# Second graph layer: the last 42 of 154 groups of edge tiles are gathered by POOL and summed by one-hot products

## The reference

```python
h = jnp.maximum(_layernorm(x, axis=-1), 0.0)
# _gcn_conv
dinv = rsqrt(degree)                      # degree of each node
h = h @ W_gcn
msg = h[src] * (dinv[src] * dinv[dst])[:, None]
features = segment_sum(msg, dst)          # sum over the edges of each dst
x = x + relu(features @ W1 + b1) @ W2 + b2
```

## Time and profile before

| | us |
|---|---|
| median of 3 runs | 7662.83 (7657.39 to 7690.72) |
| the profiled execution, its own time | 7676.02 |
| its span in the trace | 7674.2 |
| stages 1 (0 to 1130), 2 (to 5884), 3 (to 6103) | 1130, 4754, 219 |
| stage 4 (6103 to 7614) | 1511 |
| stage 5 (7614 to 7674) | 60 |

### The profile page before, as it was taken

One profiled execution on the slowest core, in us unless ns is written; L12 is line 12 of the kernel. 1 busy time (PEld: TensorE's weight loads), 2 busy tenths in 40 slices (PEclk: granted clock), 3 DMA queues, 4 the chain that ended last, 5 costly groups with the idle time before them and its releaser, 6 DMA issues. The chain is left out here.

```text
span 7674.2 us, 127785 instructions
## 1 busy us (share of the span) xinstructions
PE 5336.5 (70%) x34546; PEld 3643.4 (47%) x34546; DVE 4190.5 (55%) x13388; ACT 4709.8 (61%) x11022; POOL 3260.8 (42%) x3411
## 2 busy tenths in 40 slices
PE   7544436666666666666666666666657999999998
PEld 5211114444444444444434444444445677777777
DVE  4555564444444344444444444444445699999997
ACT  3454535555555555555555555555554499999997
POOL 3555545555555555555555555555555200000000
PEclk7555556666666666666676666666675599999998
DMA  4333322223222222232223222322232111111111
GB/s 158 105 97 93 96 72 71 70 69 87 69 69 71 85 70 69 70 88 71 71 70 88 70 71 71 86 72 69 70 87 69 37 68 68 68 68 68 68 68 69
DMA packets 315566, 586.38 MB, mean 76 GB/s; under 512 B 129522, under 2 KB 185858, under 8 KB 306546
## 3 DMA queue, kind: packets, MB, share of 16 engines
q1 hardware_dynamic: 202882, 324.53, 13.3%
q0 software_dynamic: 103344, 158.83, 9.8%
q10 hardware_dynamic: 8640, 94.84, 3.1%
HBM read 426.94 MB, written 150.87 MB: 75 GB/s over the span
## 5 line engine op out<-in xcount | busy, mean ns | idle before, releaser
L977 POOL DMA_INDIRECT gbuf<-a_tab,idxb x2688 | 2601.7, 968 | 2157.9 <-ACT idxb L968 1048.7
L1077 DVE TENSOR_TENSOR pre<-psum,gbuf 128x384 f32<-128x384 f32 x806 | 449.3, 557 | 2203.0 <-remote 1388.9
L1183 PE MATMUL psum<-x_all 128*128 128x294 bf16 x1260 | 477.8, 379 | 1367.1 <-ACT x_all L1194 860.9
L1064 PE MATMUL psum<-rhs,lhs 128*128 128x96 f32 x6448 | 1317.1, 372 | 27.0 <-ACT lhs L1038 19.8
L1064 PEld LDWEIGHTS psum<-rhs,lhs 128*128 128x128 f32 x6448 | 1202.7, 278 | 130.2 <-issue 55.7
L1108 PE MATMUL psum<-msg,oh 128*128 128x388 f32 x1612 | 1062.1, 755 | 216.2 <-ACT msg L1085 171.0
L1085 ACT ACTIVATE msg<-pre 128x384 f32<-128x384 f32 x806 | 419.9, 521 | 1282.4 <-DVE pre L1077 741.8
L1892 PE MATMUL psum<-x_all 128*128 128x294 bf16 x5208 | 1059.5, 289 | 51.6 <-DVE x_all L1885 16.2
L1183 PEld LDWEIGHTS psum<-x_all 128*128 128x128 bf16 x1260 | 142.2, 113 | 1925.1 <-issue 1032.5
L1884 DVE TENSOR_SCALAR x_all<-x_all,dstrel 128x588 bf16<-128x588 f16 x2604 | 959.4, 368 | 88.6
L1118 ACT ACTIVATE x_all<-psum 32x97 f32<-32x97 f32 x3224 | 776.7, 241 | 335.2 <-remote 245.8
(11 more groups left out here) (230 smaller groups left out, 7499.6 us busy)
## 6 DMA issues: line engine op xcount, KB each, us to landing
adj_tab<-x_all ACTq DMA_DIRECT2D x60, 1543.5 KB
gbuf<-a_tab,idxb POOLq DMA_INDIRECT x3224
x_all<-dst_row SPq DMA_DIRECT2D x806, 64.0 KB
x_all<-attr_parts SPq DMA_DIRECT2D x807, 36.0 KB
x_all<-attr_parts SPq DMA_DIRECT2D x403, 72.0 KB
x_all<-adj_tab SPq DMA_DIRECT2D x30, 945.0 KB
nf<-adj_tab SPq DMA_DIRECT2D x30, 882.0 KB
spilled<-gbuf SPq DMA_DIRECT2D x134, 192.0 KB
```

The costliest lines, as they stand in the source:

```text
L977: g.indirect_dma_start(gbuf[:, k % 4, t, :], None, a_tab[:, :], bass.IndirectOffsetOnAxis(ap=idxb[:, k % 4, t:t + 1], axis=0)).then_inc(g_ ...
L1064: ins = pe.matmul(ps_m(k)[:, t, :], lhs[:, k % 2, t * TILE:(t + 1) * TILE], rhs[:, k % 2, :], start=True, stop=True)
L1183: pe.matmul(bank[7][:, 0:HB], low_e[:, n % 2, :], key_e[:, n % 2, b * HB:(b + 1) * HB], start=True, stop=True).then_inc(n_mm, 1)
```

## The change

The last 42 groups (882 tiles, of which 872 hold edges: 218 supertiles) are no longer counted. They are the "tail". Of the other 112 groups 28 are early and 84 late, and an early group is multiplied during two of every three late groups (`w % 3 >= 1`).

* Stage 3: ACT copies each chunk's table rows from PSUM to `wide_rows` (`layer_row`), SP stores them in DRAM as `t_tab` (`layer_row_store`), and DVE's `layer_t` reads that copy. Keys are made for 2352 tiles in place of 3234.
* Stage 4: POOL gathers each tail tile's 128 rows of 32 values from `t_tab` into a ring of four supertiles (`tail_gather`). Every 8 counted tiles (`TSTEP`), DVE writes a supertile's one-hots of 32 columns (`tail_onehot`), PE multiplies the gathered rows by them in four float32 products (`tail_product`), and DVE adds 32 x 32 sums to `sT` (`tail_add`).

```diff
+TAIL = 42
+TR = 4
-        self.early = [g for g in range(4, self.NG, 5)][:self.SV // EARLY]
-        self.late = [g for g in range(self.NG) if g not in self.early]
+        self.counted = self.NG - TAIL
+        self.early = [g for g in range(3, self.counted, 4)][:self.SV // EARLY]
+        self.late = [g for g in range(self.counted) if g not in self.early]
...
+        def layer_row(act, i, k):
+            act.wait_ge(p_hid.sem, p_hid.at(c))
+            act.wait_ge(p_t.sem, p_t.at(c - 2))
+            if c >= 2:
+                act.wait_ge(o_t[k], 16 * i)
+            act.activation(t_row[:, k, :, :], ps_t(k), ACT.Copy).then_inc(p_row.sem, 1)
...
+        TSTEP = ND * GT // NTB
+        def tail_gather(g, b):
+            if b >= TR:
+                g.wait_ge(t_mm, b - TR + 1)
+            first = (d.first + b) * SUP
+            for t in range(SUP):
+                g.indirect_dma_start(g_rows[:, b % TR, t, :], None, t_tab[:, :],
+                                     bass.IndirectOffsetOnAxis(ap=src_i[:, first + t:first + t + 1], axis=0)).then_inc(t_land[b % TR], 16)
+
+        def tail_onehot(dve, b):
+            if b >= 2:
+                dve.wait_ge(t_mm, b - 1)
+            dve.tensor_tensor(o_tail[:, b % 2, :, :], iota_w.unsqueeze(1).to_broadcast([P, SUP, W]),
+                              dstrel[:, d.first + b, :].unsqueeze(2).to_broadcast([P, SUP, W]),
+                              ALU.is_equal).then_inc(t_oh, 1)
+
+        def tail_product(pe, b):
+            n = b * TSTEP
+            pe.wait_ge(t_oh, b + 1)
+            pe.wait_ge(t_land[b % TR], 16 * SUP * (b // TR + 1))
+            if n >= 3:
+                pe.wait_ge(a_ok, n - 2)
+            for t in range(SUP):
+                ins = pe.matmul(ps_tail(b), g_rows[:, b % TR, t, :], o_tail[:, b % 2, t, :], start=(t == 0), stop=(t == SUP - 1))
+            ins.then_inc(t_mm, 1)
+
+        def tail_add(dve, b):
+            n = b * TSTEP + 3
+            base = dve.value_load(base_i[:, d.first + b:d.first + b + 1], min_val=0, max_val=N - 1)
+            dve.wait_ge(t_mm, b + 1)
+            dve.wait_ge(a_ok, b * TSTEP + 1)
...
+            dve.tensor_tensor(nodes_of, nodes_of, ps_tail(b), ALU.add).then_inc(t_add, 1)
...
         def tile_counts(pe, n):
             pe.wait_ge(e_oh, n + 1)
             if n >= 3:
                 pe.wait_ge(a_ok, n - 2)
+                if tails_added(n + 1):
+                    pe.wait_ge(t_add, tails_added(n + 1))
...
+                    for b in range(NTB):
+                        tail_gather(g, b)
...
-                            if w % 4 >= 2 and w // 4 < NE:
-                                early_sums(pe, w // 4, (w % 4 - 2) * GT + j)
+                            if w % 3 >= 1 and w // 3 < NE:
+                                early_sums(pe, w // 3, (w % 3 - 1) * GT + j)
```

More of the change, by code:

```diff
@@ L58, in __init__ @@
         self.TD = GT * self.NG
-        self.early = [g for g in range(4, self.NG, 5)][:self.SV // EARLY]
-        self.late = [g for g in range(self.NG) if g not in self.early]
+        self.counted = self.NG - TAIL
+        self.early = [g for g in range(3, self.counted, 4)][:self.SV // EARLY]
+        self.late = [g for g in range(self.counted) if g not in self.early]
+        self.first = self.counted * GT // SUP
+        assert self.counted * GT % SUP == 0
+        self.NTB = self.SV - self.first
         self.NE, self.ND = len(self.early), len(self.late)
@@ L1398, in _ @@
                         ins = pe.matmul(bank[6 + b][:, 0:len(gs) * GT].rearrange("p (n j) -> p n j", j=GT), ones[0:1, :],
-                                        dst_e[0:1, gs[0]:gs[-1] + 1:5, :], start=True, stop=True)
+                                        dst_e[0:1, gs[0]:gs[-1] + 1:4, :], start=True, stop=True)
                     ins.then_inc(n_first, 1)
@@ L1508, in gnn_kernel @@
         t_rest = pre[:, :, :, 0:H]
-        KP = -(-TD // NCH)
-        key_f = dflat[:, 0:TD]
-        lo_f = src_i[:, 0:TD].bitcast(FP32)
+        TK = GT * d.counted
+        KP = -(-TK // NCH)
+        key_f = dflat[:, 0:TK]
+        lo_f = src_i[:, 0:TK].bitcast(FP32)
+        t_row = wide_rows
+        p_row = signal("p_row", 2)
+        o_t = [sem("o_t0"), sem("o_t1")]
         hi_i = rhs[:, :, :].rearrange("p b c -> p (b c)")[:, 0:KP].bitcast(I32)
@@ L1523, in tiles_of @@
         def tiles_of(c):
-            return range(c * KP, min((c + 1) * KP, TD))
+            return range(c * KP, min((c + 1) * KP, TK))
         def ps_mixed(k):
@@ L1691, in after @@
                 dve.wait_ge(q_t, 8 * c + n)
-            dve.tensor_copy(parts[0], ps_t(k)).then_inc(q_t, 1)
+            dve.tensor_copy(parts[0], t_row[:, k, :, :]).then_inc(q_t, 1)
             dve.tensor_scalar(hi, src_i[:, tiles], 7, None, ALU.logical_shift_right).then_inc(q_t, 1)
             after(1)
-            dve.tensor_tensor(rest, ps_t(k), parts[0], ALU.subtract).then_inc(q_t, 1)
+            dve.tensor_tensor(rest, t_row[:, k, :, :], parts[0], ALU.subtract).then_inc(q_t, 1)
             dve.tensor_scalar(src_i[:, tiles], src_i[:, tiles], P - 1, None, ALU.bitwise_and).then_inc(q_t, 1)
@@ L1721, in step @@
                     layer_store(sp, i, k)
-                layer.run(sp, step, 0)
+                    layer_row_store(sp, *layer.earlier(i, k, 4))
+                layer.run(sp, step, 4)
                 sp.wait_ge(p_t.sem, p_t.at(NCH - 1))
@@ L1726, in _ @@
                 sp.dma_start(nf[N % P:N % P + 1, pad:pad + C // 2], zrow[:, 0:C // 2]).then_inc(o_zero, 16)
-                sp.wait_ge(o_zero, 16)
+                for k in range(2):
+                    sp.wait_ge(o_t[k], 16 * ((NCH + 1 - k) // 2))
+                sp.dma_start(t_tab[N:N + 1, :], zrow[:, 0:H]).then_inc(o_zero, 16)
+                sp.wait_ge(o_zero, 32)
                 sp.wait_ge(o_res, 16 * NCH)
@@ L1803, in _ @@
                 act.activation(wc[:, H:H + 1], ident[0:C + 1, C:C + 1], ACT.Copy)
-                for x in (p_deg, p_col, p_own):
+                for x in (p_deg, p_col, p_own, p_row):
                     x.start(act)
@@ L1813, in step @@
                     layer_own(act, *layer.earlier(i, k, 7))
+                    layer_row(act, *layer.earlier(i, k, 7))
                 layer.run(act, step, 7)
@@ L1870, in gnn_kernel, with tails_added, late_added @@
         BJ = 7
+        NTB = d.NTB
+        TSTEP = ND * GT // NTB
+        g_rows = sq[:, :, :, :].rearrange("p b t c -> p (b t c)")[:, 0:TR * SUP * H].rearrange("p (b t c) -> p b t c", b=TR, t=SUP)
+        o_tail = oh[:, 2:4, :, :]
+        t_land = [sem(f"t_land{k}") for k in range(TR)]
+        t_oh = sem("t_oh")
+        t_mm = sem("t_mm")
+        t_add = sem("t_add")
+        def tails_added(n):
+            return min(NTB, max(0, -(-(n - 3) // TSTEP)))
+        def late_added(n):
+            return min(ND, max(0, (n - 6) // GT - 1))
@@ new lines, in tail_add @@
+        def tail_add(dve, b):
[3 more added lines that the diff above has]
+            dve.wait_ge(a_ok, b * TSTEP + 1)
+            if b >= 1:
+                dve.wait_ge(t_add, b)
+            if late_added(n):
+                dve.wait_ge(w_add, late_added(n))
+            if early_added(n):
+                dve.wait_ge(hw_add, early_added(n))
+            nodes_of = sT[0:H, bass.ds(base, W)]
+            dve.tensor_tensor(nodes_of, nodes_of, ps_tail(b), ALU.add).then_inc(t_add, 1)
@@ L1959, in group_place, with group_add @@
             pe.matmul(ps[0:H, P:2 * P], part[:, k, :], o_slot[:, k, :], start=True, stop=True).then_inc(placed, 1)
-        def group_add(dve, n, early, others):
+        def group_add(dve, n, early, at):
             ps, k, mm, summed, placed, added, groups = sums_of(early)
@@ L1967, in group_add @@
                 dve.wait_ge(added, n)
+            others = late_added(at) if early else early_added(at)
             if others >= 1:
                 dve.wait_ge(w_add if early else hw_add, others)
+            if tails_added(at):
+                dve.wait_ge(t_add, tails_added(at))
             nodes_of = sT[0:H, bass.ds(base, P)]
@@ L1994, in _ @@
                             if w < ND:
-                                tile_counts(pe, w * GT + j)
+                                n = w * GT + j
+                                if n % TSTEP == 0 and n // TSTEP < NTB:
+                                    tail_product(pe, n // TSTEP)
+                                tile_counts(pe, n)
                             if w >= 2 and j == 3:
@@ L2015, in _ @@
                     dve.wait_ge(k_v, 2)
+                    tail_onehot(dve, 0)
                     for w in range(ND + 2):
                         for j in range(GT):
+                            n = w * GT + j
                             if w < ND:
-                                edge_onehots(dve, w * GT + j)
+                                edge_onehots(dve, n)
+                            if (n + 5) % TSTEP == 0 and (n + 5) // TSTEP < NTB:
```

(8 more changed lines are left out.)

23 lines of the change are left out of this document (19 added, 4 removed).

## The result

The kernel before took 7676.77 us (median of 4 runs), the changed one 7860.81 (4 runs, 7849.86 to 7880.77): ratio 1.0244, 95% interval 1.0206 to 1.0282. The forecast was 7370. The profiled execution took 7880.77, its span is 7879.0. Two later comparisons gave 1.0219 (1.0174 to 1.0264) and 1.0202 (1.0154 to 1.0251).

The account below looks back on a forecast made before the run. Stage 4 was taken as paced by PE in groups with early blocks, otherwise ACT, with POOL free; 7676 - 285 (stage 4) - 12 (stage 2) + 4 (stage 3) = 7383 profiled, so 7370 us; range 7270 to 7590.

Parts of the forecast that it names:

- POOL: four gathers: Stage 4, POOL's gathers per step of 8 tiles: 5.0 us, taken as 5.3 with DVE's effect (5.0 to 6.3).
- engines waiting together for nothing named, as in stage 2: Stage 4: one of the signs listed as showing the forecast wrong; no size given.
- rival 3: Late landings or poor coupling: stage 2's pace of 5.9 a supertile gives 7457, POOL's upper price 7544; chance 0.15.
- Base, PE, DVE, ACT: Stage 4, per step of 8 tiles: 4.67 counting, 0.40 PE, 0.37 DVE, nothing for ACT; 5.44 us.
- DVE against POOL: Stage 4: gathers lengthen DVE's one-hots by 0.10 us each, 0.4 a step; bounds 0 and 0.18 a gather.
- The forecast of ACT's share (81%): Stage 4, sign of being right: ACT's busy share falls to some 81%, 1764 copies of 0.56 us in 1220.
- Ends: Stage 4: first product at 6109.6, when the fourth gather lands 2.6 us after issue; 26 us behind the last tail product.
- Elsewhere: Outside stage 4: stage 2 gains 12 us from fewer early tiles and stores; stage 3 loses 4 us.
- 1, gathers held back by DVE: Stage 4: gathers of 1.49 + 0.30 us make a step 7.2 with POOL the bound, total 7740; chance 0.08.
- 2, the port held for a gather: Stage 4: DVE loses 4 x 0.95 us a step, steps of 8.55, total 8030; chance 0.03.
- 4, the clock: Stage 4: PE's clock drops to 0.50 when it waits for POOL; a third of the time adds 354, total 7725; chance 0.05.
- 5, better overlap: Lower prices, steps of 5.1 us, and all of stage 2's gain: total below 7280; chance 0.07.

Follow-up runs that it names:

- the one that gathers once: Changed kernel, but POOL gathers only for the first four supertiles and the other 214 products reread those rows: 7348.21 us, ratio 0.9569.
- the singles: Changed kernel with each gather held back to its quarter of the step: 5919.46 us where the kernel before took 6233.37; 7698.64 us in another group.
- the 22 groups: Changed kernel with TAIL of 22 in place of 42, gathers singly four to five tiles apart: 7497.79 us; in bursts 7749.90 us.

## Why the prediction was wrong

**The step that failed** is the cost of the gathers: "POOL: four gathers. One takes 0.95 and the next starts 0.30 after it: 1.25, 5.0 a step". The term was right as far as it went (0.94, 1.25 apart in a burst). But besides POOL's time the prediction counted only what a gather does to DVE, and nothing of what it does to PE's signals. The runs showed in its place 7.75 - 5.32 = 2.4 us a step, 527 of the 552 us between the spans of the changed kernel and of the one that gathers once. The rest is stages 1 and 2, whose end wanders between 5842 and 5894 in the runs that met the hold.

**It could have been read.** The earlier trace rows show DVE standing for 1295 us in stage 2 for something that the profile doesn't name, and the prediction lists this sign ("engines waiting together for nothing named, as in stage 2"). In rival 3 it was taken for late landings and priced at 0.4 us a step from stage 2's pace. The trace of the kernel before has the sign in its signals: in stage 2 45% of PE's are over 0.3 us late, up to 13.7 us, in bursts of gathers longer than four; in stage 4, without gathers, none. The group that didn't meet the hold prices it: stages 1 and 2 last 4379 us there against 5821. So the kernel before loses some 1440 us where the hold is met, all of it in the stages with gathers, and the changed kernel 527 more in stage 4. (The 4379 are of the singles; the kernel before has no trace from that group, but its time differs by the same 1440.)

**Base, PE, DVE, ACT** (5.44 a step, 5.5 coupled): 5.32 measured without gathers, 5.35 with gathers that hold nothing. "PE's and DVE's extra waits ask for things that the rings of three give anyway" holds. "DVE against POOL", taken as 0.4 a step, is 0.17: DVE works 1031 us in stage 4, and 993 with the first ring's gathers alone. The forecast of ACT's share (81%) was off in itself: a copy keeps ACT busy for 0.61 us and not for the 0.56 of its pace, and the kernel that gathers once has 1073 of 1192, 90%.

**Ends.** First product at 6109.1 (forecast 6109.6), 25.5 us behind the last (26). The first is luck: the gathers began 3 us before the forecast's 6103.3, and the fourth one's rows were on hand 4.7 us after it started, not 2.6 (later ones have a median of 2.4).

**Elsewhere.** Stage 3: 212.8 us against 213.0, where +4 was taken. Stage 2: -12 was taken, and the traces end it 3 us apart, far inside its spread; not settled.

**Rivals.** 1, gathers held back by DVE: no, 0.99 us on average. 2, the port held for a gather: no; line 1982 has a median of 370 ns beside gathers and 356 without. The rule about the port that the prediction weighed isn't what decides here. (Whether line 1982's instructions are in the two-port mode that it speaks of, no run shows.) The Trainium skill, "SBUF — State Buffer", in the same section "Who interferes with whom", also states that TensorE and ScalarE never wait on anyone. For ScalarE's signals the trace agrees (none late). PE's signals came up to 5.0 us late beside gathers, and PE stood up to 1.1 us before products that wait for nothing. The section is about SBUF's ports, and no run shows whether a port has to do with this; but it can't be read as saying that POOL's work leaves PE alone, and there the measurement decides. 3, late landings: the rows lay ready 23 us early; its time was too low. 4, the clock: at 0.50 for 314 us of the stage, but as a follower. What it added to the stalls wasn't separated. (The rival's sum uses 4.64 and 0.7 where the prediction's own terms are 4.67 and 0.6; with these it comes to some 7710.) 5, better overlap: true of the work (5.32), void for the whole.

**Settled and open.** Shown: gathers alone bring the loss, the added work doesn't; bytes, POOL's time and plain transfers by POOL don't; bursts are worse than the same number apart. Only argued: that the signal is held while the product is done. The ends of products in the trace are modelled, so they don't prove it. For it speaks that PE's next products had started, and that 338 of 1648 signals of `a_mm` stand less than 0.2 us behind the last one, where the kernel before and, behind its first ring, the one that gathers once have never less than 0.25. That PE itself stands at such times says that more than a signal can be held. Open: what holds the signals, whether the look-up or the scattered rows of a gather matter, why one group of runs was free of it, and whether the change as it is would be faster there (its form with single gathers was, by 5%).

## What to carry to other kernels

An engine with nothing to do isn't free if what it would do disturbs the others: price a new kind of instruction from a stage that already has it, by that stage's pace and by every wait in it that nothing explains, and not from its own duration. When engines stand still together behind a product that is recorded as done, look when its signal was raised. If gathers on POOL must run beside a loaded PE, place them singly with a microsecond or two between them (the 22 groups: 7498 us against 7750 in bursts), and compare kernels only within a group of runs.

## What the runs showed of the hardware

- PE's signals are raised up to 5.0 us behind the recorded end of the product (13.7 in stage 2 of the kernel before) while POOL issues gathers close behind each other. Behind gaps of 1 to 2 us few are late: 12% with 42 groups, none of 925 with 22 (but 6% behind gaps over 2 us).
- PE also stands, up to 1.1 us at a time and 58 us in stage 4 of the changed kernel, before products that no semaphore holds back. It never does so in the kernels without gathers there, nor in the group of runs free of the hold.
- Transfers of the same size, of consecutive rows, written out by POOL without look-up (0.53 us each) or by SP (1.8 us from issue to landing) hold nothing, nor does POOL's own work of 1001 us in 1212.
- The number of rows of a gather hardly matters: 0.87 us for 32 (one run), 0.94 for 128, and as many signals late.
- The same kernel took 6233 us in one group of runs and in five others 7668 to 7686 (medians). In that group's traces the stage without gathers was as long as elsewhere (stage 3: 214 us).
